# Gate and up products of an expert block with the weights stationary and the rows streamed

## The reference, cut to what matters

```
logits = xf @ router_w.T
top_logits, top_idx = top_k(logits, 2)
top_w = softmax(top_logits)
for e in range(8):
    w_e = sum(top_w * (top_idx == e))
    h = silu(xf @ Wg[e].T) * (xf @ Wu[e].T)      # 192 -> 768
    out = out + h @ Wd[e].T * w_e[:, None]       # 768 -> 192
```

## Time and profile before

| | |
|---|---|
| median of 3 runs | 297.85 us (297.75 to 298.26) |
| span of the profiled execution | 295.3 us |
| TensorE busy, mean granted clock | 199.8 us (68%), 0.80 |
| VectorE, ScalarE, GpSimd busy | 218.4, 122.2, 137.1 us |
| expert layer, first product to last copy | 183.2 to 281.8 us |

### The profile page before, as it was taken

The page is one execution under the profiler, slowest core; times in us unless marked ns, Lnnn a source line. Parts: engine busy times, 40 slices in busy tenths (PEclk is TensorE's granted clock), DMA queues, the critical chain, the costliest instruction groups (busy, mean ns, idle before and its releaser), DMA issues.

```text
span 295.3 us, 4727 instructions
## 1 busy us (share of the span) xinstructions
PE 199.8 (68%) x1320; PEld 163.6 (55%) x1333; DVE 218.4 (74%) x522; ACT 122.2 (41%) x265; POOL 137.1 (46%) x150
## 2 busy tenths in 40 slices
PE   0999658297499312837637203999999999999700
PEld 0999647297499301727637102577666666676500
DVE  2599999898899898989898989573555455555404
ACT  0544371380571216847546572343433333343300
POOL 7799992283466164735375687702112111211210
PEclk9999999669598855555555555899999999999965
DMA  6999303999204009526666642231111101111023
GB/s 244 415 338 392 145 0 124 350 389 207 37 2 146 2 10 312 148 82 183 196 208 219 165 133 63 82 89 33 44 44 39 47 31 49 31 47 33 16 87 120
DMA packets 21821, 39.14 MB, mean 133 GB/s; under 512 B 4872, under 2 KB 11560, under 8 KB 21288
## 3 DMA queue, kind: packets, MB, share of 16 engines
q1 hardware_dynamic: 20392, 36.12, 37.8%
q0 software_dynamic: 1408, 2.76, 2.9%
HBM read 33.56 MB, written 5.30 MB: 132 GB/s over the span
## 4 chain that ended last, share of the span: by engine, by line
DVE 53%; PE 31%; DMA 6%; issue 6%; ACT 2%; SPq 2%; DVEq 0%; POOLq 0%; ACTq 0%
DVE rs L695 5%; DVE rs L696 5%; DVE rs L694 4%; PE ps L1191 4%; DVE h L756 4%; PE ps L1189 4%; DMA experts<-w_proj 4%; PE ps L1194 3%; PE ps L1193 3%; DVE experts L345 3%; PE ps L1201 3%; DVE shared L827 3%; PE ps L1190 2%; PE ps L1215 2%; PE ps L1216 2%
## 5 line engine op out<-in xcount | busy, mean ns | idle before, releaser
L1017 PE MATMUL ps<-experts 128*117 128x193 f32 (+1 forms) x320 | 62.7, 359 | 14.0 <-DVE experts L728 7.5
L1017 PEld LDWEIGHTS ps<-experts 128*117 128x117 f32 (+1 forms) x320 | 59.8, 203 | 15.0 <-DMA experts<-x_t 14.6
L345 POOL TENSOR_TENSOR experts<-stage,experts 128x528 bf16<-128x528 f32 x43 | 49.8, 1187 | 37.1 <-ACT experts L520 37.1
L465 POOL TENSOR_TENSOR experts<-experts 128x468 f32<-128x468 f32 x35 | 52.3, 1493 | 26.8 <-ACT experts L506 24.7
L944 DVE TENSOR_TENSOR shared<-shared,ps 128x256 f32<-128x256 f32 x48 | 20.2, 422 | 43.3 <-ACT shared L636 40.4
L487 POOL DMA_INDIRECT pair_y<-shared x16 | 15.6, 972 | 76.1 <-DVE shared L964 55.4
L520 ACT CAST experts<-stage 128x528 f16<-128x528 f32 x64 | 37.6, 628 | 18.2 <-DMA stage<-w_exp 18.0
L636 ACT ACTIVATE shared<-ps 128x256 f32<-128x256 f32 x48 | 18.4, 384 | 56.6 <-PE ps L1194 55.4
L506 ACT ACTIVATE experts<-experts 128x468 f32<-128x468 f32 x40 | 22.8, 590 | 25.9 <-POOL experts L465 18.1
L1215 PE MATMUL ps<-experts,shared 128*128 x96 | 23.6, 246 | 2.0 <-DVE shared L949 1.6
L1216 PE MATMUL ps<-experts,shared 128*128 x96 | 23.6, 246 | 0.0
(11 more groups left out here) (182 smaller groups left out, 379.5 us busy)
## 6 DMA issues: line engine op xcount, KB each, us to landing
stage<-w_exp SPq DMA_DIRECT2D x64, 264.0 KB, 3.3
experts<-x_t SPq DMA_DIRECT2D x4, 1888.0 KB, 13.5
experts<-w_proj SPq DMA_DIRECT2D x4, 768.0 KB, 7.6
shared<-slot_x SPq DMA_DIRECT2D x16, 128.5 KB, 2.1
slot_x<-experts SPq DMA_DIRECT2D x1, 2048.0 KB, 20.4
experts<-x_t SPq DMA_DIRECT2D x4, 472.0 KB, 8.3
yy<-pair_y SPq DMA_DIRECT2D x2, 351.0 KB
out<-h SPq DMA_DIRECT2D x2, 175.5 KB
```

What stands on the lines that cost most here:

```text
L345: ops.tensor_tensor(lo_w[:, to + EW:to + EW + PW], stage[:, n % STAGES, :], hi_w[:, to:to + PW], ALU.subtract).then_inc(split_pool if on_p ...
L465: g.tensor_tensor(acc, acc, sq[:, added % 2], ALU.add).then_inc(sq_used, 1)
L1017: last = mm(dst, xbuf[:, t % 2, k, 0:m], gw[:, k, :], start=k == 0, stop=k == KT - 1)
```

## The change

The gate and up products swap sides: the weights are stationary, 128 columns at a time, and the chunk's rows are streamed. The result then comes out as units by slots, so that hid needs no transpose: turn_hidden, its semaphore and its two PSUM banks go, and hidden_high and hidden_low read hid from SBUF. Steps are of 384 units, two to a chunk. A step's gate and up have a bank each (banks 0 and 1, 2 and 3), two pairs in turn, so gate_up waits for the product two steps back. The down projection stays two steps behind, which are now longer steps. turn_rows and rows_high move from r = 1 to r = 0, finish from r = 2 to r = 1; the waits on hidT_done become waits on hidT_ready, and hidden_high waits for down two steps back.

```
-    BLK = 256
+    BLK = 384
...
-        Y_BANKS = (3, 6)
+        Y_BANKS = (4, 6)
...
-                a.activation(act[:, s % 2, :], pcol(s % 3, 0, BLK), ACT.Silu).then_inc(act_ready, 1)
+                a.activation(act[:, s % 2, :], pcol(2 * (s % 2), 0, BLK), ACT.Silu).then_inc(act_ready, 1)
 
             def hidden_high(n, s):
-                sc.wait_ge(hidT_done, n + 1)
-                a.copy(hh[:, s % 2], pcol(4 + s % 2, 0, BLK).rearrange("p (h t) -> p h t", h=HT)).then_inc(hh_ready, 1)
+                sc.wait_ge(hid_ready, n + 1)
+                if not (isinstance(n, int) and n < 2):
+                    sc.wait_ge(down_step, n - 1)
+                a.copy(hh[:, s % 2], hid[:, s % 2, :].rearrange("p (h t) -> p h t", h=HT)).then_inc(hh_ready, 1)
...
-                    if r == 1 and not (last and j == 3):
+                    if r == 0 and not (last and j == 3):
                         rows_high(c0 + (j + 1), j + 1)
...
-                    dve.wait_ge(hidT_done, n - 1)
-                v.tensor_tensor(hid[:, s % 2, :], act[:, s % 2, :], pcol(s % 3, BLK, BLK), ALU.mult).then_inc(hid_ready, 1)
+                    dve.wait_ge(hidT_ready, n - 1)
+                v.tensor_tensor(hid[:, s % 2, :], act[:, s % 2, :], pcol(2 * (s % 2) + 1, 0, BLK), ALU.mult).then_inc(hid_ready, 1)
...
-                v.tensor_tensor(hl[:, s % 2], pcol(4 + s % 2, 0, BLK).rearrange("p (h t) -> p h t", h=HT), hh[:, s % 2],
+                v.tensor_tensor(hl[:, s % 2], hid[:, s % 2, :].rearrange("p (h t) -> p h t", h=HT), hh[:, s % 2],
                                 ALU.subtract).then_inc(hidT_ready, 1)
...
-                dve.wait_ge(down_done, c + 1)
+                dve.wait_ge(down_step, STEPS * (c + 1))
...
-                    if r == 2 and not (first and j == 0):
+                    if r == 1 and not (first and j == 0):
...
             def gate_up(n, s, off):
-                if not (isinstance(n, int) and n < 3):
-
-                    pe.wait_ge(hid_ready, n - 2)
+                if not (isinstance(n, int) and n < 2):
+
+                    pe.wait_ge(hid_ready, n - 1)
                 j, r = divmod(s, STEPS)
-                dst = pcol(s % 3, 0, 2 * BLK)
-                k1, k2 = 2 * BLK * r, W2 + 2 * BLK * r
-                mm(dst, x1h[:, j % 2, 0, :], part_w(0, off, k1, 2 * BLK), start=True, stop=False)
-                mm(dst, x1h[:, j % 2, 0, :], part_w(1, off, k1, 2 * BLK), start=False, stop=False)
-                mm(dst, x1l[:, j % 2, :], part_w(0, off, k1, 2 * BLK), start=False, stop=False)
-
-                mm(dst, x1h[:, j % 2, 1, :], part_w(0, off, k2, 2 * BLK), start=False, stop=False)
-                mm(dst, x1h[:, j % 2, 1, :], part_w(1, off, k2, 2 * BLK), start=False, stop=True).then_inc(gu_done, 1)
-
-            def turn_hidden(n, s):
...
-                for h in range(HT):
-                    last = tr(pcol(4 + s % 2, h * P, P), hid[:, s % 2, h * P:(h + 1) * P], ident[:, :])
-                last.then_inc(hidT_done, 1)
+                for b in range(2 * HT):
+                    dst = pcol(2 * (s % 2) + b // HT, b % HT * P, CHUNK)
+                    k1, k2 = 2 * BLK * r + b * P, W2 + 2 * BLK * r + b * P
+                    mm(dst, part_w(0, off, k1, P), x1h[:, j % 2, 0, :], start=True, stop=False)
+                    mm(dst, part_w(0, off, k1, P), x1l[:, j % 2, :], start=False, stop=False)
+                    mm(dst, part_w(1, off, k1, P), x1h[:, j % 2, 0, :], start=False, stop=False)
+
+                    mm(dst, part_w(0, off, k2, P), x1h[:, j % 2, 1, :], start=False, stop=False)
+                    last = mm(dst, part_w(1, off, k2, P), x1h[:, j % 2, 1, :], start=False, stop=True)
+                last.then_inc(gu_done, 1)
...
-                if r == STEPS - 1:
-                    last.then_inc(down_done, 1)
+                last.then_inc(down_step, 1)
...
                     gate_up(n0 + s, s, off)
-                    if not (first and s < 1):
-                        turn_hidden(n0 + (s - 1), s - 1)
-                    if r == 1 and not (last and j == 3):
+                    if r == 0 and not (last and j == 3):
                         turn_rows(c0 + (j + 1), j + 1)
```

More of the change, by code:

```diff
@@ L317, in vit_tower @@
         hid_ready = sem("hid_ready")
-        hidT_done = sem("hidT_done")
         hh_ready = sem("hh_ready")
         hidT_ready = sem("hidT_ready")
-        down_done = sem("down_done")
+        down_step = sem("down_step")
         y_ready = sem("y_ready")
@@ L971, in round4 @@
                         hidden_low(n0 + (s - 1), s - 1)
-                    if r == 1 and not (last and j == 3) and not (first and j + 1 < FIRST):
+                    if r == 0 and not (last and j == 3) and not (first and j + 1 < FIRST):
                         rows_low(c0 + (j + 1), j + 1)
                     if first and j < FIRST - 2:
-                        pick(j + 2, r)
-                    if r == 2 and not (first and j == 0):
+                        for step in range(r, 2 * r + 1):
+                            pick(j + 2, step)
+                    if r == 1 and not (first and j == 0):
                         if j == 0:
-                            dve.wait_ge(down_done, c0)
+                            dve.wait_ge(down_step, c0 * STEPS)
                             dve.wait_ge(y_out[1], 8 * c0 - 16)
@@ L1182, in gate_up @@
             def gate_up(n, s, off):
-                if not (isinstance(n, int) and n < 3):
-                    pe.wait_ge(hid_ready, n - 2)
+                if not (isinstance(n, int) and n < 2):
+                    pe.wait_ge(hid_ready, n - 1)
                 j, r = divmod(s, STEPS)
-                dst = pcol(s % 3, 0, 2 * BLK)
-                k1, k2 = 2 * BLK * r, W2 + 2 * BLK * r
-                mm(dst, x1h[:, j % 2, 0, :], part_w(0, off, k1, 2 * BLK), start=True, stop=False)
-                mm(dst, x1h[:, j % 2, 0, :], part_w(1, off, k1, 2 * BLK), start=False, stop=False)
-                mm(dst, x1l[:, j % 2, :], part_w(0, off, k1, 2 * BLK), start=False, stop=False)
-                mm(dst, x1h[:, j % 2, 1, :], part_w(0, off, k2, 2 * BLK), start=False, stop=False)
-                mm(dst, x1h[:, j % 2, 1, :], part_w(1, off, k2, 2 * BLK), start=False, stop=True).then_inc(gu_done, 1)
-            def turn_hidden(n, s):
-                pe.wait_ge(hid_ready, n + 1)
-                if not (isinstance(n, int) and n < 2):
-                    pe.wait_ge(hidT_ready, n - 1)
-                for h in range(HT):
-                    last = tr(pcol(4 + s % 2, h * P, P), hid[:, s % 2, h * P:(h + 1) * P], ident[:, :])
-                last.then_inc(hidT_done, 1)
+                for b in range(2 * HT):
[7 more added lines that the diff above has]
+                last.then_inc(gu_done, 1)
             def down(c, n, s, off):
@@ L1256, in _ @@
             down(CHUNKS - 1, S - 2, S - 2, offset(1))
-            turn_hidden(S - 1, S - 1)
             down(CHUNKS - 1, S - 1, S - 1, offset(1))
@@ L1265 @@
     from concourse.bass_utils import run_bass_kernel_spmd
-    P, PATCH, SEQ, IMGS, TILES, BLK = 128, 32, 9, 13, 5, 256
+    P, PATCH, SEQ, IMGS, TILES, BLK = 128, 32, 9, 13, 5, 384
     x = np.asarray(x)
```

## The result

The changed kernel takes 347.08 us (median of 4 runs, 346.16 to 347.81), the kernel before on the same chip 297.80 (4 runs, 297.45 to 298.26): a ratio of 1.165 (1.160 to 1.170), 49.3 us slower. The profiled execution took 347.81 us, with a span of 346.0 against 295.3. The forecast was 341 us with a range of 330 to 359, and the likeliest mechanism was the right one.

What follows compares the result with a forecast made beforehand. Issue of weight addresses on TensorE's queue was to become the bound: addresses 115.9, other instructions 19.2, edges 2.4 and cold start 0.4 make 137.9 against 94.2 us; +43.7, tail -0.7, span 338.3, plus 2.55 gives 341 us, range 330 to 359.

Steps and rivals of the forecast that it cites:

- the likeliest mechanism: Gate and up loop: issue of weight addresses on TensorE's queue becomes the bound, 341 us; chance 73%.
- The bound now: Loop over 16 chunks before the change: runs at TensorE's array pace, 5.59 us a chunk, address work hidden.
- Array after: TensorE's array after the change: 60 pairs of 0.057 us, 5.14 us a chunk, 0.45 less than before.
- Rival (b): Gate and up: a load and product pair can't follow faster than 0.082 us, so 314 us; chance 3%.
- Price of an address: TensorE's queue: each new register address for expert weights costs 0.123 us before the product that uses it.
- Rival (a): Lines 1189 to 1194: address work doesn't hold the array, so the change is faster, 290 us; chance 8%.
- Rival (d): Weight loads with register addresses cost one more register instruction each, 115 us more, 456 us; chance 4%.
- Rival (c): Loop bound by issue and TensorE's clock falls too: 359 us wholly at low clock, 350 half; chance 12%.
- New waits free: Waits of down and gate_up on other engines' products cost nothing: down needs them over 4 us after ready.
- The sum: Loop to the last gate and up product: 137.9 us against 94.2, +43.7; with the tail, 341 us.
- edges of the loop: At the loop's edges a step starts later than usual: 0.8 x 3 = 2.4 us in all.
- The tail: From the last gate and up product to the final copy: 3.4 us instead of 4.1, -0.7.

Runs made afterwards that it cites:

- down_one: Changed kernel with the down projection one step of 384 behind the gate and up products instead of two: 399.81 us, ratio 1.345.
- down_one_turned: As down_one, with hidden_high of the step before ahead of silu on ScalarE and hidden_low ahead of gate on VectorE: 344.38 us, ratio 1.162.
- one_copy: Changed kernel with the offset copied once a chunk for gate_up and once for down instead of at each step: 345.26 us.
- copied: Changed kernel with VectorE copying three of four gate and up weight parts to fixed places one chunk ahead: 296.24 us, ratio 0.997.
- both padded kernels: Changed kernel and copied, each with 48 more register instructions at the head of TensorE's queue: 346.72 and 296.43 us.
- fixed_gu: Changed kernel with gate and up weights always of expert 0, at fixed addresses: 291.46 us, ratio 0.982.
- two_addr: Changed kernel with two weight addresses a block instead of four, high parts used in place of low: 298.40 us, ratio 1.005.
- five_addr: Changed kernel with a fifth weight address a block, line 1193 reading columns of its own: 367.59 us, ratio 1.239.
- steps_256: Changed kernel with steps of 256, three to a chunk, weights still stationary: 348.56 us.
- copied_padded: As copied, with 48 more register instructions at the head of TensorE's queue: 296.43 us, ratio 0.999.

## Why the prediction was right, and where its numbers failed

**The bound now.** TensorE in the loop, as read. That fixed addresses gave the kernel before only 0.7 us confirms that its queue was covered.

**Array after.** 0.057 us a pair from the picks gave 5.14 us a chunk; with fixed addresses it is 5.06 in the steady chunks. Rival (b), 0.082 us, is excluded by the loads 0.055 apart. The Trainium skill (TensorE: Matmul & The Clock Gate, "Wait — 56ns, not 53.3ns?") gives 55.6 ns at full clock and 106.7 cold for products of 128 columns, and the trace agrees (0.28 / 5 = 0.056, 0.53 / 5 = 0.106); the 81 ns of its section on the issue gap, on which (b) leant, is not met, although each product here has a load of its own.

**Price of an address.** 0.123 us from the earlier trace rows. Blocks of 0.497 us at the median, 0.124 for the fifth address of a block and 0.120 between two and five addresses all bear it out. The mean is a little higher, 0.513 / 4 = 0.128, and that matters for the sum below. Rival (a) fell, and with it the reading of the Trainium skill's rule (Advanced Engine Details and Errata, Sequencer and Instruction Queues) that queued instructions run on beside a control instruction: they may be read, but the product behind each address came 0.12 us late.

**A load with a computed address** cost nothing above a streamed operand with one: loads of lines 1192 and 1193 are 0.01 apart. Rival (d) is out.

**The clock.** Rival (c) feared it would fall. Three windows of 10 us:

```profile
190.00:200.00 10.00, 7.27 (x82) 6.42 (x82) 5.13 (x9) 3.35 (x9) 1.74 (x2) 0.83 0.31 89
200.00:210.00 10.00, 9.75 (x109) 7.73 (x105) 3.71 (x8) 2.33 (x6) 0.98 (x1) 1.00 0.07 20
...
220.00:230.00 10.00, 8.95 (x85) 7.16 (x84) 2.81 (x7) 2.29 (x7) 0.97 (x1) 0.83 0.09 25
```

After 190 us it fell twice and came back, and was 1.00 in the other windows up to 330. So the sign that the prediction named for (c) came, and its price did not. The falls cost little, since at half clock a block takes the array's 0.53 us, 0.03 more than its addresses.

**New waits free.** True of the time, for a reason that the prediction gave only in half. It said that down needs a product two steps later, over 4 us after it is ready. It did not say that by the order on ScalarE one step would be too little however long the step is. The distance was load-bearing, worth 53 us. And where the issue of addresses is gone, a cover is gone too: with fixed addresses the first chunks take 6 to 7 us, and among their waits TensorE waits 2.2 us for the 0/1 matrices that VectorE makes for the picks (line 861).

**The sum.** Span +50.7 us against +43.0. By places: the first load was at 183.66, 0.5 us later than the first product of the earlier trace rows. From there to the end of the last gate and up product (328.15 + 0.23) are 144.7 us, where the sum had 137.9. Of these 6.8, 3.4 lie ahead of the first silu (190.25 - 183.66 = 6.6; 24 addresses and a handover are 3.2). 2.8 are in the 15 chunks from there to the silu at 324.16 (133.9 against 15 x 8.58 + 2.4 = 131.1): **the term that was too small is the 0.123 us for an address of gate and up**. An ordinary chunk took 8.81 us on average, not 8.58. Its twelve blocks make up 12 x 0.513 = 6.16 where the sum had 48 x 0.123 = 5.90, which covers the difference; what is left, 8.81 - 6.16 = 2.65, is the 12 addresses of down (1.48) and 1.2 for the other register and semaphore instructions, as forecast. The median block is as forecast too: the excess comes from single steps of 0.14 to 0.28 us between addresses, and why these are longer stays open. The three edges of the loop took some 0.5 us more in all than the 2.4 forecast, and the first chunk, 7.63 us, gives back about 1.2 of the late start. The last 0.6 are in the last step. The tail, 328.38 to the copy at 332.06, is 3.7 instead of 3.4: TensorE did two down steps there, the first of which had also waited for the low parts behind the last gate:

```profile
328.94 0.56 DVE L945 TENSOR_TENSOR shared<-shared,ps 128x384 f32<-128x384 f32 x1 [3.23 <-ACT shared L635]
329.41 0.55 DVE L950 TENSOR_TENSOR shared<-shared 128x384 bf16<-128x384 f32 x1
...
330.10 0.25 PE L1211 MATMUL ps<-experts,shared 128*128 x1 [0.72 <-DVE shared L950]
330.98 0.10 PEld L1211 LDWEIGHTS ps<-experts,shared 128*128 128x128 f16 x1
...
332.06 0.36 DVE L965 COPY shared<-ps 128x192 f32<-128x192 f32 x1 [1.36 <-PE ps L1213]
```

That is the same order that down_one uncovered, and it stood in the code to be read.

**The signs.** The patterns of 0.01 and 0.12 and blocks of 0.50 came, chunks in the range of 8.4 to 8.9 but for the edges and the first, and longer waits of ScalarE and VectorE. One sign of being right did not come: TensorE shows hardly any idle time that could be put down to issue. From 190.25 to 328.8 it shows as busy 129.5 of 138.6 us, for the shown ends overlap. Whoever had gone by it would have read "bound by the array". And one sign of being wrong did seem to come, TensorE waiting for VectorE's hid:

```profile
248.56 0.23 PE L1192 MATMUL ps<-shared,experts 128*128 128x128 f16 x1 [0.28 <-DVE shared L945]
```

It stands at the start of nearly every chunk, twelve times and 4.7 us from 196 to 320 us. By the code this product needs the gate of two steps back, and the one that ends just before it (247.88 + 0.55 = 248.43) is of the step before. What stands in between on TensorE's queue are the register instructions of a new chunk: the views of lines 1223, 1224 and 1187 have four of them between 247.97 and 248.36. So this is issue put down to another engine, and it is the same in down_one_turned (4.2 us, twelve times).

## What to carry to other kernels

An operand slice at a run-time offset costs an instruction on the queue of the engine that uses it, and that is free only as long as the work per address is longer than its issue: here 0.22 us of array per address hid 0.12, and 0.08 did not. Making operands smaller, as one does when weights become stationary, multiplies addresses while the arithmetic stays the same, so count the instructions of the queue as well as those of the array. Before moving a step nearer to its producer, write down what stands ahead of each producer in its own queue: with down one step behind, the order of two lines on ScalarE and VectorE was worth 55 us, more than the whole change, and with down two steps behind it had hidden its price.

## What was not expected of the hardware

Between about 187 and 193 us, in the changed kernel, its repetition, one_copy, down_one, copied and both padded kernels, ScalarE's first silu starts some 3 us or more after its product, in a wait the trace calls remote, and TensorE's queue stops for 0.6 to 1.5 us at a time; in fixed_gu, two_addr, five_addr, steps_256 and down_one_turned the first silu comes at once (185.87 to 186.89). The silu starts 3.2 us after the end of its last product in five of these kernels and 4.7 in copied and copied_padded; of the 3.2 the next chunk gives back some 1.2. The wait that the trace shows, from the end of ScalarE's table load, is as constant: 6.50 to 6.54 us in the five, 7.99 and 7.97 in the two. It repeats for a program, does not change when TensorE's code is moved by 48 instructions, and down_one_turned, which differs from down_one only in the order of a few instructions, lacks it. GpSimd issues its scatters of the rows there and the DMA engines are busy 0.31 of the time from 190 to 200 us, but no run separated these from it: its cause stays open. So does that of the single steps between addresses that take 0.14 to 0.28 us instead of 0.12 (240.66 to 240.80 above, and 241.68 to 241.95 in the same step).
